# A Mamba block with a SwiGLU behind it on one core: GpSimd's products two blocks at a time, and the beats set anew

## What is computed

```python
x_in, res = split(x @ W_in)                       # 512 each
u = silu(causal_dw_conv(x_in, conv_w, conv_b))    # 4 taps
dt, B, C = split(u @ W_x, [16, 32])               # 16 states
delta = softplus(dt @ W_dt + b_dt)
h = exp(delta * A) * h + (delta * u) * B          # for each of 512 channels x 16 states, over time
y = sum_n(h * C) + u * D
x = layernorm(x + (y * silu(res)) @ W_out)
x = layernorm(x + (silu(x @ wg.T) * (x @ wu.T)) @ wd.T)
```

## Time and profile before

| | before |
|---|---|
| median of 3 runs | 1806.37 us (1805.71 to 1807.34) |
| the profiled execution | 1807.88 us, span 1806.0 us |
| TensorE | 1682.5 us busy, 93% |
| VectorE | 1691.4 us, 94% |
| ScalarE | 1617.7 us, 90% |
| GpSimd | 1593.9 us, 88% |

### The profile page before, as it was taken

How to read it: one execution, slowest core, us unless ns; L and a number is a source line. 1 busy time by engine, 2 the same in 40 slices (tenths; PEclk the granted TensorE clock), 3 DMA queues, 4 the chain that set the end, 5 groups by cost and what they waited for, 6 DMA issues and landing times.

```text
span 1806.0 us, 32054 instructions
## 1 busy us (share of the span) xinstructions
PE 1682.5 (93%) x10112; PEld 1262.6 (70%) x10112; DVE 1691.4 (94%) x1965; ACT 1617.7 (90%) x2784; POOL 1593.9 (88%) x1374
## 2 busy tenths in 40 slices
PE   8879899999999999899998999999899998999878
PEld 3556676776767677676776767677676776767668
DVE  4989999999999999999999999999999999999997
ACT  4898989899899998989899898998989899898876
POOL 2889799898989989899898989989899898989973
PEclk9999999999999999999999999999999999999999
DMA  7323123222222223223222222323213222221110
GB/s 243 117 71 117 48 82 115 74 106 82 104 85 82 107 90 117 77 75 113 83 106 75 103 93 73 116 78 119 87 64 124 84 106 72 92 96 48 47 47 25
DMA packets 82119, 164.52 MB, mean 91 GB/s; under 512 B 10385, under 2 KB 28049, under 8 KB 81954
## 3 DMA queue, kind: packets, MB, share of 16 engines
q1 hardware_dynamic: 80514, 160.90, 25.5%
q10 hardware_dynamic: 1440, 1.58, 0.3%
HBM read 87.47 MB, written 8.91 MB: 53 GB/s over the span
## 4 chain that ended last, share of the span: by engine, by line
PE 68%; ACT 20%; issue 5%; POOL 4%; DVE 3%; DMA 0%; DVEq 0%; SPq 0%; ACTq 0%; POOLq 0%
PE ht_upper L766 10%; PE ht_lower L766 10%; PE y_upper L791 9%; PE fill L588 8%; PE fill L702 8%; PE fill L692 6%; PE fill L671 6%; PE fill L603 3%; POOL dbu L1290 3%; ACT gt L1147 3%; ACT da L1138 3%; ACT L1213 2%; ACT da_ahead L1138 2%; ACT L1225 2%; PE fill L641 2%
## 5 line engine op out<-in xcount | busy, mean ns | idle before, releaser
L1290 POOL TENSOR_TENSOR dbu<-du,brep 128x512 f32<-128x512 f32 x1024 | 1297.0, 1299 | 162.5 <-DVE h L1492 137.5
L1492 DVE TENSOR_TENSOR_SCAN h<-da,h,dbu 128x512 f32<-128x512 f32 x720 | 888.9, 1269 | 36.3 <-ACT da L1138 34.0
L1138 ACT ACTIVATE da<-delta,a_s 128x512 f32<-128x512 f32 x960 | 659.9, 694 | 56.6 <-DVE h L1492 53.3
L1147 ACT ACTIVATE gt<-ht_upper,ct 128x512 f32<-128x512 f32 x512 | 351.1, 686 | 71.5 <-PE ht_upper L766 67.1
L766 PEld LDWEIGHTS ht_upper<-ident,h 128*128 128x128 f32 x2048 | 243.0, 142 | 195.7 <-issue 124.0
L766 PE MATMUL ht_upper<-ident,h 128*128 128x128 f32 x2048 | 314.5, 276 | 70.0 <-ACT gt L1147 53.9
L1505 DVE SCALAR_TENSOR_TENSOR acc<-ht_lower,ct,acc 128x512 f32<-128x512 f32 x480 | 350.9, 731 | 7.8 <-PE ht_lower L766 6.4
L766 PE MATMUL ht_lower<-ident,h 128*128 128x128 f32 x2048 | 313.0, 276 | 23.0 <-DVE acc L1505 19.1
L766 PEld LDWEIGHTS ht_lower<-ident,h 128*128 128x128 f32 x2048 | 240.1, 142 | 98.8 <-DVE h L1492 47.9
L791 PE MATMUL y_upper<-ident,gt 128*128 128x128 f32 x2048 | 308.6, 274 | 0.0
L1492 DVE TENSOR_TENSOR_SCAN h<-da,dbu 128x512 f32<-128x512 f32 x240 | 282.5, 1209 | 19.9 <-ACT da L1138 19.1
(11 more groups left out here) (200 smaller groups left out, 1906.3 us busy)
## 6 DMA issues: line engine op xcount, KB each, us to landing
brep<-b_rows SPq DMA_DIRECT2D x127, 512.0 KB, 3.7
xs<-xin SPq DMA_DIRECT2D x242, 256.0 KB, 2.5
xr<-x SPq DMA_DIRECT2D x16, 512.0 KB, 3.9
xt_s<-x_t SPq DMA_DIRECT2D x15, 512.0 KB, 3.8
out<-xr SPq DMA_DIRECT2D x15, 512.0 KB, 2.8
win_s<-w_in SPq DMA_DIRECT2D x2, 512.0 KB, 5.2
h<-xin SPq DMA_DIRECT2D x4, 256.0 KB, 4.2
h<-xin ACTq DMA_DIRECT2D x4, 256.0 KB, 4.6
```

The costliest lines, as they stand in the source:

```text
L1138: nc.scalar.activation(dst[:, :], delta[:, par, m, :], ACT.Exp, scale=a_s[:, m, n:n + 1])\
L1147: nc.scalar.activation(gt[:, (n * UPPER + k) % GT, :], ht_upper[:, :], ACT.Copy, scale=ct[:, par, k, n:n + 1])\
L1290: nc.gpsimd.tensor_tensor(dbu[:, beat % DBU, :], du[:, par, m, :], brep[:, n // PIECE % 2, n % PIECE, :], ALU.mult).then_inc(dbu_ready, 1)
L1492: nc.vector.tensor_tensor_scan(h_times(i, n, m, 0, T), da[beat % 2][:, :] if slot is None else da_ahead[:, slot, :], dbu[:, beat % DBU, :] ...
```

## The change

- GpSimd multiplies two channel blocks by one row of B in one instruction (128x1024), at even beats. The four products of state 0 in chunk 0 stay single. dbu has 6 buffers instead of 4; HOLD becomes (3, 2), by which products 35 and 46, and so the pairs (34, 35) and (46, 47), wait for scans 33 and 45.
- GpSimd widens the float16 part of x1, at its beats 29 and 33, in place of ScalarE at 29 and 35.
- da_ahead is gone. The exponentials ahead go to xs[0] and xs[1], the buffer of the tap rows of the convolution. They wait for the last convolution of the next chunk, and SyncE's first tap DMA of a chunk waits for scan 45 of the chunk in which they stood.
- The second session begins at 43.0 instead of 43.5. Silu of z is two instructions of two blocks each, at 32.0 and 32.5; in chunk 0 too, where it was in the second session. Silu of u is at 32.0 instead of 31, behind the gt and the z copy of beat 31.5.
- At the start only the row of state 0 goes through TensorE and VectorE, into the da[0] bank; state 1 comes by a DMA of its own from b_rows. dtb is read ahead of the exponential of a_log, and ct behind dt2.
- 40 steps have other beats. A path by which GpSimd multiplies by up is there, but with MOVED = () it issues nothing.

Of the tables only the entries with new beats are shown.

```diff
-FILL_AT: xin3 (5, 7), yt0 (6,), conv0 (10,), o2 (17, 17, 17, 18), o3 (18, 18, 18, 18), conv2 (19,), res0 (20, 20),
-  gate0 (32, 35), gate2 (36, 37), res3 (32, 33), up0 (40, 44), dtb (42, 42, 43, 43), up3 (47, 47), up5 (49, 49),
-  down0 (53, 53, 53, 53, 53, 54), down2 (57, 59, 59, 59, 59, 60), xin0 (-9, -9)
+FILL_AT: xin3 (6, 8), yt0 (5,), conv0 (9,), o2 (16, 17, 17, 18), o3 (17, 18, 18, 18), conv2 (20,), res0 (19, 20),
+  gate0 (31, 34), gate2 (36, 36), res3 (31, 33), up0 (41, 44), dtb (41, 42, 43, 43), up3 (47, 48), up5 (50, 50),
+  down0 (52, 52, 52, 52, 52, 53), down2 (57, 59, 59, 59, 59, 61), xin0 (-10, -9)
-READ_AT: xin0 -6.5, res0 25, xin1 2, conv1 16, res2 32.5, dt1 50.5, dt3 54, yt0 8, o1 14.5, x1t0 27.5, x1t1 29.5,
-  gate0 36, up0 45.5, gate1 37, up4 48, up5 50, down1 59.5, down2 61.5
+READ_AT: xin0 -7, res0 24, xin1 2.5, conv1 16.5, res2 31.5, dt1 50, dt3 54.5, yt0 9, o1 15, x1t0 27, x1t1 30.5,
+  gate0 37, up0 45, gate1 37.5, up4 49, up5 50.5, down1 60.5, down2 63
-BEAT: soft exp [48.5, 51, 56.5, 56.5], soft ln [49, 51.5, 57, 59.5], add u [52, 55, 60, 63], times u [53, 56, 63, 63],
-  x1 cut [29, 35], x1 low [30.5, 31.5], y upper [5.5, 6.5], times z [8, 11, 13, 17], rstd [22, 79], shift [24, 90],
-  norm [(25, 26, 26, 26), (94, 100, 104, 104)], halo -23.5, silu uz [31, 32.5], silu gate [43.5, 45]
+BEAT: soft exp [49, 51, 56.5, 57.5], soft ln [49.5, 51.5, 57, 60.5], add u [52, 55, 58, 62], times u [55, 56, 63, 63],
+  x1 cut [29, 33], x1 low [29.5, 31.5], y upper [6.5, 7], times z [10, 12, 12, 16], rstd [22, 81.5], shift [24, 93],
+  norm [(24, 25, 25, 25), (95, 102, 106, 106)], halo -24.5, silu a [31, 32.5], silu b [43, 45],
+  silu at [32, 32, 32.5, 44, 45]
-AHEAD = 2
-DBU = 4
-HOLD = (0, 3)
+AHEAD = (('xs0', 'xs1'), ('xs0', 'xs1'))
+DBU = 6
+HOLD = (3, 2)
...
-            def times_b(i, par, beat):
+            def times_b(i, par, beat, blocks):
                 n, m = beat // DB, beat % DB
                 if n == 0:
-                    pool.wait_ge(du_ready, i * DB + m + 1)
+                    pool.wait_ge(du_ready, i * DB + m + blocks)
...
-                after(pool, h_ready, i * NH + max(used, HELD.get(beat, used)) + 1)
-                nc.gpsimd.tensor_tensor(dbu[:, beat % DBU, :], du[:, par, m, :],
-                                        brep[:, n // PIECE % 2, n % PIECE, :], ALU.mult).then_inc(dbu_ready, 1)
+                for b in range(beat, beat + blocks):
+                    used = b - DBU if b >= DBU else max(other for other in range(NH) if other % DBU == b % DBU) - NH
+                    after(pool, h_ready, i * NH + max(used, HELD.get(b, used)) + 1)
+                b_row = brep[:, n // PIECE % 2, n % PIECE:n % PIECE + 1, :]
+                nc.gpsimd.tensor_tensor(dbu[:, beat % DBU:beat % DBU + blocks, :], du[:, par, m:m + blocks, :],
+                                        b_row if blocks == 1 else b_row.broadcast_to([P, blocks, T]),
+                                        ALU.mult).then_inc(dbu_ready, blocks)
...
+            def widen(c, k):
+                pool.wait_ge(high_cut, c * KK + k + 1)
+                nc.gpsimd.tensor_copy(x1t[:, 0, k, :], high16(k)).then_inc(high_ready, 1)
...
-                    times_b(i, par, beat)
+                    if first and beat < DB:
+                        times_b(i, par, beat, 1)
+                    elif beat % 2 == 0:
+                        times_b(i, par, beat, 2)
...
-                for k in tiles_due("x1 cut", beat):
-                    act.wait_ge(high_cut, c * KK + k + 1)
-                    copy(x1t[:, 0, k, :], high16(k)).then_inc(high_ready, 1)
...
-            def silu_z(c, par):
-                act.wait_ge(res_raw, c * DB)
-                nc.scalar.activation(z[:, par, :, :], z[:, par, :, :], ACT.Silu).then_inc(z_ready, 1)
+            def silu_z(c, par, half):
+                blocks = slice(half * DP, (half + 1) * DP)
...
+                nc.scalar.activation(z[:, par, blocks, :], z[:, par, blocks, :], ACT.Silu).then_inc(z_ready, 1)
```

More of the change, by code:

```diff
@@ L24 @@
 SILU_SET = "silu_and_others"
-FILL_AT = {"xin2": (2, 2), "xin3": (5, 7), "yt0": (6,), "yt1": (9,), "conv0": (10,), "o0": (10, 10, 13, 13),
[8 rows of a table removed]
+FILL_AT = {'xin3': (6, 8),
+ 'yt0': (5,),
+ 'yt1': (9,),
+ 'conv0': (9,),
+ 'xin2': (2, 2),
+ 'o0': (10, 10, 13, 13),
+ 'o2': (16, 17, 17, 18),
+ 'o1': (13, 13, 14, 14),
+ 'conv1': (14,),
+ 'o3': (17, 18, 18, 18),
+ 'conv2': (20,),
+ 'res0': (19, 20),
+ 'res1': (23, 24),
+ 'x1t1': (28,),
+ 'x1t0': (26,),
+ 'conv3': (26,),
+ 'res2': (31, 31),
+ 'gate3': (38, 38),
+ 'gate0': (31, 34),
+ 'gate2': (36, 36),
+ 'res3': (31, 33),
+ 'gate1': (35, 35),
+ 'up1': (45, 45),
+ 'gate5': (39, 39),
+ 'up0': (41, 44),
+ 'gate4': (38, 38),
+ 'dtb': (41, 42, 43, 43),
+ 'up2': (45, 45),
+ 'dt0': (45,),
+ 'ct': (45,),
+ 'up3': (47, 48),
+ 'dt1': (49,),
+ 'up4': (48, 48),
+ 'up5': (50, 50),
+ 'down0': (52, 52, 52, 52, 52, 53),
+ 'dt2': (50,),
+ 'dt3': (51,),
+ 'down1': (55, 56, 57, 57, 58, 58),
+ 'down2': (57, 59, 59, 59, 59, 61),
+ 'down3': (62, 62, 62, 62, 62, 62),
+ 'xin1': (-1, 0),
+ 'xin0': (-10, -9)}
 FILLS = list(FILL_AT)
 FRONT = ("xin", "conv", "res", "dtb", "ct", "dt")
-BANK = {"xin2": 1, "xin3": 0, "yt0": 1, "yt1": 1, "conv0": 0, "o0": 1, "o1": 0, "conv1": 1, "o2": 1, "o3": 0,
[4 rows of a table removed]
+BANK = {'xin2': 1,
+ 'xin3': 0,
+ 'yt0': 1,
+ 'yt1': 1,
+ 'conv0': 0,
+ 'o0': 1,
+ 'o1': 0,
+ 'conv1': 1,
+ 'o2': 1,
+ 'o3': 0,
+ 'conv2': 0,
+ 'res0': 1,
+ 'res1': 0,
+ 'x1t0': 1,
+ 'conv3': 0,
+ 'x1t1': 0,
+ 'res2': 1,
+ 'gate0': 0,
+ 'res3': 1,
+ 'gate1': 1,
+ 'gate2': 0,
+ 'gate3': 1,
+ 'gate4': 0,
+ 'gate5': 1,
+ 'up0': 1,
+ 'dtb': 0,
+ 'up1': 0,
+ 'up2': 1,
+ 'dt0': 0,
+ 'ct': 1,
+ 'up3': 1,
+ 'up4': 0,
+ 'dt1': 1,
+ 'up5': 0,
+ 'dt2': 1,
+ 'dt3': 0,
+ 'down0': 1,
+ 'xin0': 0,
+ 'down1': 1,
+ 'down2': 0,
+ 'down3': 1,
+ 'xin1': 0}
 F_FILLS = sorted((name for name in FILLS if name.rstrip("0123456789") in FRONT), key=lambda name: FILL_AT[name][-1])
@@ L58 @@
 GT = 4
-READ_AT = {"xin0": -6.5, "conv0": 13.5, "res0": 25, "xin1": 2, "conv1": 16, "res1": 26, "xin2": 4.5, "conv2": 23,
[5 rows of a table removed]
[L67 to L71, removed]
+READ_AT = {'xin0': -7.0,
+ 'conv0': 13.5,
+ 'res0': 24,
+ 'xin1': 2.5,
+ 'conv1': 16.5,
+ 'res1': 26,
+ 'xin2': 4.5,
+ 'conv2': 23,
+ 'res2': 31.5,
+ 'xin3': 9,
+ 'conv3': 28.5,
+ 'res3': 35,
+ 'dtb': 45,
+ 'ct': 47,
+ 'dt0': 48.5,
+ 'dt1': 50.0,
+ 'dt2': 52.0,
+ 'dt3': 54.5,
+ 'yt0': 9,
+ 'yt1': 10.0,
+ 'o0': 13.5,
+ 'o1': 15.0,
+ 'o2': 19,
+ 'o3': 19,
+ 'x1t0': 27.0,
+ 'x1t1': 30.5,
+ 'gate0': 37,
+ 'up0': 45.0,
+ 'gate1': 37.5,
+ 'up1': 45.5,
+ 'gate2': 38.5,
+ 'up2': 45.5,
+ 'gate3': 39.5,
+ 'up3': 48,
+ 'gate4': 40,
+ 'up4': 49,
+ 'gate5': 41,
+ 'up5': 50.5,
+ 'down0': 54,
+ 'down1': 60.5,
+ 'down2': 63.0,
+ 'down3': 63}
+BEAT = {'soft exp': [49.0, 51, 56.5, 57.5],
+ 'soft ln': [49.5, 51.5, 57, 60.5],
+ 'add u': [52, 55, 58, 62],
+ 'times u': [55, 56, 63, 63],
+ 'x1 cut': [29, 33],
+ 'x1 low': [29.5, 31.5],
+ 'y upper': [6.5, 7.0],
+ 'times z': [10, 12, 12, 16],
+ 'mean': [21, 64],
+ 'rstd': [22, 81.5],
+ 'shift': [24, 93],
+ 'square': [(21, 21, 21, 21), (64, 65, 67, 76)],
+ 'norm': [(24, 25, 25, 25), (95, 102, 106, 106)],
+ 'halo': -24.5,
+ 'silu a': [31, 32.5],
+ 'silu b': [43.0, 45],
+ 'silu at': [32, 32.0, 32.5, 44.0, 45],
+ 'times up': [49, 47, 50, 50, 53, 55]}
 FIRST_FILLS = ["xin0", "xin1", "xin2", "xin3", "conv2", "conv0", "conv1", "conv3", "dtb", "dt0", "dt1", "ct", "dt2", "dt3"]
@@ L698, in down @@
                 if t == 0:
[L699 removed]
+                    pe.wait_ge(*hid_done(c, n))
                 if n == 0:
@@ L1230, in step @@
                 for beat in range(NH):
-                    if ahead(beat) is None and beat not in AFTER_SILU and not (first and beat < 2):
+                    if beat not in PLACES and beat not in AFTER_SILU and not (first and beat < 2):
                         exp(i, par, beat)
@@ L1343, in step @@
                             normalise(i - 2, par, which, t)
+                    for k in [] if first else tiles_due("x1 cut", beat):
+                        widen(i - 1, k)
+                    for m in [] if first else tiles_due("times up", beat):
+                        if m in MOVED:
+                            times_up(i - 1, m)
                     for k in [] if first else tiles_due("times z", beat):
```

239 lines of the change are left out of this document (146 added, 93 removed), and 17 rows, old and new, of tables (BANK, FILL_AT, READ_AT).

## The result

| | before | after |
|---|---|---|
| median | 1806.86 us (6 runs, 1805.71 to 1811.24) | 1819.01 us (6 runs, 1817.74 to 1821.95) |
| ratio of the times | | 1.0067, 95% interval 1.0055 to 1.0079 |
| profiled execution | 1807.88, span 1806.0 | 1817.74, span 1815.8 |

The prediction said 1801.8 with a range up to 1809.5. The change costs 12 us, 0.67%. The two profiled executions lie 9.9 us apart, and what follows adds up to that. The one after is the fastest of its six; the other five have a mean granted clock of 0.988 to 0.992, against its 0.992, so most of them had more time at half clock, but where is not on record.

What follows compares the result with a forecast made beforehand. No engine bounds the whole span; TensorE's time counts wherever it doesn't wait. Start 0.7 + boundary 0.9 + 15 chunks x 0.2 = 4.6 off the median 1806.37 gives 1801.8 us; range 1790 to 1809.5.

Steps and rivals of the forecast that it cites:

- the part on ScalarE: Moved x1 copies, halved silu z and new order in session one sum to 0; the copy gone at beat 35 gives 0.2.
- Other beats: Moved fills, y upper, yt, times z: TensorE's work between the same two points is unchanged and unbroken, so 0 each.
- The 0.2 from the copy at beat 35: Scan 36's wait of 0.27 behind ScalarE's x1 copy goes, bringing session two earlier: 0.2 us a chunk taken.
- rival 1: TensorE bounds also behind session two, or z halves cost scan 36's gain: only the start's 0.7 left, 1805.7; chance 0.25.
- Silu z of chunk 0: Moving it from session two to session one: -1.9 and +2.1, counted as 0.
- Start: One row of B through TensorE and VectorE; exp 0's idling and ct read go: 0.7 earlier, ends 0 and 1.3.
- sign of a first scan near 32.6: Listed among what would show the forecast: the kernel's first scan near 32.6.
- Boundary: Between chunks 0 and 1, VectorE's wait of 1.74 for the first product shrinks: gain 0.9, ends -1.1 and 1.7.
- TensorE's waiting in session one: Sign of the forecast: TensorE's idle time in the first Silu session is still 4.4.
- rival 2: ScalarE's relief reaches the chain: 0.94 a chunk, 15.7 in all, 1790.7; sign: scan 34 under 12.4 after scan 28; chance 0.20.
- The chunk of 108.5: Sign of the forecast: a chunk period of 108.5 by the first scans of two chunks.
- Rival 3: Slower: GpSimd's second widening runs into scan 32, delaying later scans up to 0.6 a chunk, +7.4, 1813.8; chance 0.13.

Runs made afterwards that it cites:

- experiment 2: Changed kernel with 16 unread transposes filling TensorE's wait behind beat 33, exp 35 waiting for them: 1812.71 us, 1.0032 of the kernel before.
- Experiment 3: Kernel before the change, with only silu u moved to beat 32, behind the first gt: 1813.88 us, 1.0036 of the kernel before.
- Experiment 8: Changed kernel with five first-quarter beats (xin3, yt0 and its read, conv0, upper y) put back as before: 1817.58 us, 1.0055 of the kernel before.
- experiment 7: Changed kernel with only the conv0 fill put back from beat 9 to 10: 1817.49 us, 1.0059 of the kernel before.
- Experiment 5: Changed kernel with silu z of chunk 0 alone back in the second session: 1815.27 us, 1.0045 of the kernel before.
- experiment 6: Changed kernel with one GpSimd product an instruction everywhere, six buffers and holds kept: 1818.65 us, 1.0064 of the kernel before.

## Why the prediction was wrong

**The step that failed** is in the part on ScalarE: that gt and the z copy before silu u free TensorE's first wait, "but it has the same work up to beat 33 and then waits longer for the gt behind exp 34: 0". All that it says of the order happened: 1.33 and 2.26 in place of 1.51 and 1.22, at the same period. What it left out is the clock. I read the granted clock of 1.00 in the window rows as a property of the kernel, while it hung on how TensorE's waiting was cut up. No rival had it. It cost 5 x 1.6 = 8 us in the profiled execution, 6.3 by experiment 2, and 7 when it was made alone in the kernel before. Experiment 3 changes only the order, and experiment 2 only fills the wait; together they show the cause. Either alone would leave a rival: that the new order costs something else, or that the added work helps in another way.

**Other beats, "0 each"**, failed by 0.2 a chunk. That the same work stands between two points isn't enough: a fill that covered a wait of 0.24 for the scan went behind it, and in a stretch where TensorE has no slack that idle time is lost. Experiment 8 shows it, 108.89 to 108.63, but for all five beats at once; which of xin3, yt0 and the upper y it takes is open, and conv0 alone isn't it (experiment 7).

**The 0.2 from the copy at beat 35**: scan 36 no longer waits, as said, and scan 36 gains 0.34 on scan 34. It is given back at scan 40, which waits for TensorE's ht_lower, as from 57 us on TensorE runs without a break. Of the 0.2, 0.07 is left in experiment 8. This is close to rival 1, TensorE as the bound, only that it is so already ahead of session two. The row of 20.99 busy of 21.20 us had said so.

**Silu z of chunk 0, "-1.9 and +2.1, 0"**: the two don't cancel, because they meet different waits. In the first session the 2 us lie ahead of exp 34, and scan 34 waits 2.82 for it; in the second scan 46 waits for the held pair that begins only behind scan 45, so the 1.9 taken away there gives nothing. Experiment 5: 1.84 in chunk 0.

**Start**: 1.34 against 0.7, and 32.1 to 32.6 in the other kernels with the changed start. It was the other end, 1.3. The prediction didn't agree with itself here: its sign of a first scan near 32.6 (32.55 measured) fits that end and not the 0.7 of its sum, which gives 33.2. **Boundary**: -0.9 was expected, the wait grew by 0.48. With chunk 0 put right it is 1.27 instead of 1.74 (experiment 5): half of the gain is there.

**What held**: TensorE's waiting in session one (4.66 with the 1.07 ahead of it, 4.4 expected) and scan 34 at 12.65 behind scan 28, so no sign of rival 2; a pair takes 2.376 (2.4 was taken), pairs are worth 0 (experiment 6), scans 32 and 33 aren't stretched, the hold costs nothing in chunks 1 to 14, session one as such is worth 0, and scan 36 doesn't wait. The chunk of 108.5 didn't come, it is 108.89. Rival 3 had the right side for the wrong reason: the widening takes 0.630, not 1.1, and runs into nothing. Rival 2 didn't come.
